# Two products and a convolution read from PSUM, and a softmax scaled on ScalarE instead of GpSimd, in a two-layer network

## The reference

```python
x = x + gla(xn) + local(xn)                  # xn = layernorm(x)
x = x + delta(xn) + moe(xn)                  # xn = layernorm(x)

# local attention, in windows of 64 queries, 8 heads, twice
attn = softmax(where(mask, -max, bq @ bk.T)); out = attn @ bv

# delta: short convolution, then per chunk of 32 tokens, for two gates w_l and w_g
q = silu(sum(xp[:, j:j + L, :] * w[:, j] for j in range(4)))      # k and v alike
u = T @ v_c;  wm = T @ kb_c
u_i = (u_i - wm_i @ S) * w_i[..., None]
o_i = q_i @ S + a @ u_i;  S = S + k_i.T @ u_i

# moe: 8 heads x 8 experts, gates from a top-2 routing
v = einsum('bshep,bshe->bhsp', x @ v_w, gate_v)
ctx = softmax(q @ k.T) @ v;  out = einsum over experts of (ctx * gate_o) @ o_w
```

## Time and profile before

| what | us |
|---|---|
| runs: median, lowest, highest | 1290.52, 1286.07, 1291.62 |
| the profiled execution | 1297.51 |
| its span | 1295.0 |
| PE, DVE busy | 1175.6, 971.2 |
| ACT, POOL busy | 721.9, 851.1 |

### The profile page before, as it was taken

The page is one execution under the profiler, slowest core; times in us unless marked ns, Lnnn a source line. Parts: engine busy times, 40 slices in busy tenths (PEclk is TensorE's granted clock), DMA queues, the critical chain, the costliest instruction groups (busy, mean ns, idle before and its releaser), DMA issues.

```text
span 1295.0 us, 31167 instructions
## 1 busy us (share of the span) xinstructions
PE 1175.6 (91%) x11890; PEld 930.8 (72%) x11890; DVE 971.2 (75%) x1950; ACT 721.9 (56%) x2060; POOL 851.1 (66%) x1157
## 2 busy tenths in 40 slices
PE   5778799899999798899999999989999898989898
PEld 3455477777678677777778777877688776878686
DVE  5858799876995969877687977968768956865354
ACT  5787876458655562567456665437666533332322
POOL 3746466686787727787568754887639876865841
PEclk9999989999999999999999999999999999999999
DMA  6111165555376438764566563775348565767673
GB/s 255 34 38 34 37 237 191 167 192 163 100 242 207 139 105 264 233 200 130 178 205 210 153 193 124 265 243 171 101 135 262 185 220 183 268 223 250 222 249 125
DMA packets 91186, 230.87 MB, mean 178 GB/s; under 512 B 9888, under 2 KB 16160, under 8 KB 90912
## 3 DMA queue, kind: packets, MB, share of 16 engines
q1 hardware_dynamic: 90896, 228.30, 54.3%
q10 hardware_dynamic: 144, 0.59, 0.1%
HBM read 225.71 MB, written 3.15 MB: 177 GB/s over the span
## 4 chain that ended last, share of the span: by engine, by line
PE 32%; DVE 24%; ACT 5%; DMA 4%; issue 3%; POOL 0%; DVEq 0%; ACTq 0%; POOLq 0%
PE bank L899 8%; PE bank L946 6%; DVE ogate L1352 5%; PE bank L827 3%; PE bank L936 2%; DVE dy L1210 2%; DVE kv L1123 2%; DMA kv<-values 2%; PE bank L612 2%; PE bank L917 1%; PE bank L927 1%; DVE mmin L1341 1%; PE bank L647 1%; DMA ogate<-gates 1%; PE bank L671 1%
## 5 line engine op out<-in xcount | busy, mean ns | idle before, releaser
L1748 POOL TENSOR_TENSOR vgate<-vgate,xT 128x512 f32<-128x512 f32 x256 | 330.3, 1313 | 102.4 <-DMA vgate<-gates 102.1
L899 PE MATMUL bank<-wv,vgate 128*128 128x128 f32 x2048 | 257.5, 280 | 6.4 <-DVE prob L1055 2.4
L899 PEld LDWEIGHTS bank<-wv,vgate 128*128 128x128 f32 x2048 | 245.3, 194 | 17.4 <-issue 5.2
L946 PE MATMUL bank<-ogate,wo 128*128 128x256 f32 x1024 | 244.4, 385 | 7.7 <-DVE ogate L1352 6.7
L946 PEld LDWEIGHTS bank<-ogate,wo 128*128 128x128 f32 x1024 | 189.8, 191 | 40.6 <-issue 14.3
L1352 DVE TENSOR_TENSOR ogate<-ogate,bank 128x1024 f32<-128x1024 f32 x128 | 152.9, 1212 | 33.3 <-PE bank L936 30.3
L1463 ACT ACTIVATE prob<-prob,mx 128x128 f32<-128x128 f32 (+1 forms) x256 | 96.0, 377 | 53.7 <-DVE mx L1059 53.4
L1681 POOL TENSOR_TENSOR rot<-rot 128x512 f32<-128x512 f32 x64 | 81.6, 1275 | 56.6 <-DVE rot L1035 56.2
L1630 ACT ACTIVATE mprob<-bank,mmin 128x256 f32<-128x256 f32 x128 | 59.2, 468 | 104.3 <-DVE mmin L1341 104.1
L1724 POOL TENSOR_TENSOR step<-dlt,uw 128x126 f32<-128x126 f32 (+22 forms) x248 | 92.5, 373 | 24.7 <-DVE dlt L1275 8.7
L1726 POOL TENSOR_TENSOR dlt<-dlt,step 128x126 f32<-128x126 f32 (+22 forms) x248 | 95.4, 385 | 19.4
(11 more groups left out here) (227 smaller groups left out, 2493.1 us busy)
## 6 DMA issues: line engine op xcount, KB each, us to landing
vgate<-gates SPq DMA_DIRECT2D x128, 512.0 KB, 4.5
ogate<-gates SPq DMA_DIRECT2D x128, 512.0 KB, 4.2
wv<-in_wv_moe SPq DMA_DIRECT2D x128, 256.0 KB, 4.8
wo<-in_wo_moe SPq DMA_DIRECT2D x128, 256.0 KB, 4.6
kv<-values SPq DMA_DIRECT2D x64, 256.0 KB, 4.5
local<-in_local SPq DMA_DIRECT2D x1, 1715.0 KB, 10.6
wqkv<-in_wqkv SPq DMA_DIRECT2D x2, 768.0 KB, 7.0
x<-in_x SPq DMA_DIRECT2D x8, 128.0 KB, 5.3
```

The lines of the kernel that those rows point to most:

```text
L899: i = nc.tensor.matmul(out[:, n * D:(n + 1) * D], xg[:, e, n * P:(n + 1) * P], m.wv[slot][:, e, :], start=(q, n, e) == (0, 0, 0), stop=(q, ...
L946: i = nc.tensor.matmul(out[:, 0:T], m.wo[slot][:, e, :], cg[:, e, :], start=(h, q, e) == (0, 0, 0), stop=(h, q, e) == (MH - 1, 1, EQ - 1))
L1748: i = tt(gate[:, e:e + half, :], gate[:, e:e + half, :], spread(m.xT[b % 2][:, :], 1, half), ALU.mult)
```

## The change

The convolution reads the products in their PSUM banks: DVE's first instruction multiplies the whole row by the last tap, and each later tap adds to the columns from 1, 2 or 3 on, so that neither `pad` nor its zeros are needed. ACT's three copies go; two products share a bank, so that `din` takes two banks instead of three. In the recurrence DVE multiplies `uw` by the gates' weights as it copies it from PSUM (w u - (w wm) S is w (u - wm S)), ACT's copy goes, and so does the second product of each chunk. The local softmax is scaled on ACT, by four instructions of one scale per row, where POOL had one multiplication. All turns and banks are written anew; the numbers of stages are the same, but for the pieces that come and go.

```diff
 TENSOR_TURNS = (
-    "GaaaaGGGaaaaabbXababbbbaGbababbabacaaacabGGbcacabGGcbbbaaabGbbaabbaaabbbGGaGcbGabcbbbcbcbGcbbGabaacaacGaaacbbc"
+    "GaaaaaGGGaaaaaGaaaaaXaabbababbbaabbbbaaababbabababbaacaGcbcabGbcbGababbbGbaaGbGaaaaabbGaabbaaabbabbcbbcbcbbbbc"
...
-         "fT": 1, "fsel": 1, "din": 3, "l2": 1, "dgate": 1, "kk": 1, "uw": 1, "du": 1, "ds": 1,
+         "fT": 1, "fsel": 1, "din": 2, "l2": 1, "dgate": 1, "kk": 1, "uw": 1, "du": 1, "ds": 1,
...
     def din(b):
-        for k in range(3):
-            bank = banks.of("din", b, i=k)
+        for i, kinds in enumerate(((0, 1), (2,))):
+            bank = banks.of("din", b, i=i)
             out = take(bank)
             x_ready(b)
-            nc.tensor.matmul(out[:, 0:T], m.w_delta[:, k, :], m.xT[b % 2][:, :], start=True, stop=True).then_inc(bank.filled, 1)
+            for at, k in enumerate(kinds):
+                last = nc.tensor.matmul(out[:, at * T:(at + 1) * T], m.w_delta[:, k, :], m.xT[b % 2][:, :], start=True, stop=True)
+            last.then_inc(bank.filled, 1)
...
     def conv(b, k):
-        raw = banks.of("din", b, i=k)
-        v.wait_ge(raw.emptied, raw.use)
-        v.wait_ge(s.zeroed1, 1)
+        bank = banks.of("din", b, i=k // 2)
+        raw, out = filled(bank)[:, k % 2 * T:(k % 2 + 1) * T], m.dy[b % 2][:, k, :]
...
-        v.chain(ts(m.dy[b % 2][:, k, :], m.pad[:, k, 0:T], m.conv[:, k, 0:1], None, ALU.mult))
-        for j in range(1, CONV):
+        v.chain(ts(out, raw, m.conv[:, k, CONV - 1:CONV], None, ALU.mult))
+        for late in range(1, CONV):
             v.settle()
-            i = stt(m.dy[b % 2][:, k, :], m.pad[:, k, j:j + T], m.conv[:, k, j:j + 1], m.dy[b % 2][:, k, :], ALU.mult, ALU.add)
-            if j < CONV - 1:
+            i = stt(out[:, late:], raw[:, 0:T - late], m.conv[:, k, CONV - 1 - late:CONV - late], out[:, late:], ALU.mult, ALU.add)
+            if late < CONV - 1 or k == 0:
                 v.chain(i)
-        i.then_inc(s.conv, 1)
+            else:
+                i.then_inc(bank.emptied, 1)
...
+    def uw(b, half):
+        bank = banks.of("uw", b, half)
+        v.wait_ge(s.dw, nth("dgates", b))
+        rows = m.uw[:, half * NC_:(half + 1) * NC_, :, :].rearrange("p c a t -> p c (a t)")
+        tt(rows, chunks(filled(bank)), spread(m.gates[b % 2][:, 2 + half, :], 2, 2 * CH), ALU.mult).then_inc(bank.emptied, 1)
...
         tt(m.dlt[:, c, :, :], u4[:, c, :, :], out, ALU.subtract).then_inc(bank.emptied, 1)
-        v.wait_ge(bank.emptied, bank.use)
-        tt(m.dlt[:, c, :, :], m.dlt[:, c, :, :], spread(m.gates[b % 2][:, 2:4, c], 2, CH), ALU.mult).then_inc(s.du, 1)
...
             e = act(p[:, c, :], p[:, c, :], ACT.Exp, scale=-1.0, bias=top[:, c:c + 1], accum_out=rsum[:, c:c + 1])
         e.then_inc(s.sexp, 1)
+        yield
+        a.wait_ge(s.ssum2, nth("score", b, l, w))
+        for c in range(LH // 2):
+            e = act(p[:, c, :], p[:, c, :], ACT.Copy, scale=rsum[:, c:c + 1])
+        e.then_inc(s.snorm, 1)
...
-    def din(b):
-        for k in range(3):
-            bank = banks.of("din", b, i=k)
-            act(m.pad[:, k, CONV - 1:], filled(bank)[:, 0:T], ACT.Copy).then_inc(bank.emptied, 1)
...
-    def uw(b, half):
-        bank = banks.of("uw", b, half)
-        act(m.uw[:, half * NC_:(half + 1) * NC_, :, :], filled(bank).rearrange("p (c a t) -> p c a t", c=NC_, a=2),
-            ACT.Copy).then_inc(bank.emptied, 1)
...
-    def score(b, l, w):
-        p, rsum = prob_of(m, b, l, w)[:, :, 0:keys_of(w)], sums_of(m, b, l, w)[1]
-        g.wait_ge(s.ssum2, nth("score", b, l, w))
-        tt(p, p, spread(rsum[:, :], 2, keys_of(w)), ALU.mult).then_inc(s.snorm, 1)
```

More of the change, by code:

```diff
@@ new lines @@
+    "VDDaVDDaDGAbbaDDVbbGaVbcbAaADGcVbbVbbDAcDPbbPbbAGGbEPcPcGAzAVaAVaaCaACPFPPAAVAVPPAcAAVAaVaaaaAFFCPPAAVaAaVGGDA"
+    "DGbDbDGcDPDDAAcbPcADDPFcbbbzPADVAAVCDDACbbDbPDDVDVDDAbbDAbAcCDDADVcDDGGVcDFcDADPPcEAAVAFFFPVAPaPaaaAAVAaPaVaAa"
+    "aAPAVAPaPaAbbAAaAPVPAbbAAVAaaDbbVDbaaAbaaabDGDVabbDVbaDDcGDDGbbPDcAADVADDVcbPAcDDGDcDDbDbbaDDbDPDDAAaVaADaVGbb"
+    "GAGGaDDPbbPbAcAVcAVcVPAPaPAcAVGAaPGcVAaAzAaEAVPPaVAGPAAabAaPGGbaAaGAAPAbVbPGCDVbbFAVAACDAbPbaDbFFFVaDPAabbAAGb"
+    "DDVcADPcDDGCDaADDcacDPbDDAbDaPcDbDDVDDaDVDDADzAPVbAbbDACVCPbbAEbAGDVVPAbbAbAVAcVcPAPFAAcVAVaPcaaaPPAcAAVCVGAaa"
@@ new lines @@
+    "aGcGcaaabcccaacbbzCCabbFFFCCCbCCFCCaAaCFFAaabGFFaabGGaaaFGGGGbabbcGGVVGGbaOOAacVAVGGacaVVDDcccOOAcbAzCDCbabaaC"
+    "CCbaVVOAOACCGGCbCcGbbVcVCbbcOObGVVbAFbAFFFOOcccVVcDAcAccOOaVaAVAaaGOOcccAcAaGaOOAFFbAaabbDDDGDFFbDGDbDFGGbaDaV"
+    "VGGDaDODaDODAGGAabDGaGbDVDVDaaDGGGGbVVbbGcGbGGDcDcbDVVbbADDbADOEGOcccacazOCOACAGVaVaCCCaaOCCOAFAVFVFCOOFACVAVC"
+    "aaFFcaaODOAAVGVDDDbDDbbcDGcDGGObGOGGGcAccDGFAFcFzbCDGbCOODVVACbDCbADCDCCCDVCVCDOcDODAcDAcVDVDFDcccFDFDDEcFOGOA"
+    "GFAFaFaFVVFaaOOaaAGGAGGVaaVGOaaOGAAbObbAOAabVVabODOAbAaDaVVDbDaabDaDaDVVDcDbGDbbcDObOAcDAVVccDcDGDcbDDbbDaDaOb"
@@ new lines @@
+GPSIMD_TURNS = (
+    "aaaaaaaaGGGaGaaGaGGaaGaaGaaaaaaGaaGGGGGGGaaaGaaaaaaaaaaaGaaGWWWGGWWWaaWaWaWGGDDaDaaWWaDGWDWDWWGDDDWWaWaWaaaGaa"
+    "aDDDDWaDaGDaDDWaDDGGaDGDDaWDaaWGDGWWGGWWDDDDDDWDWaWaWaaDWDaaaaGWWWDDDDGGGDDGDWWDDDDWWDDDDWWDDDDDaaWaaWDaaaaDWD"
+    "WDWGWaaaaGWaDaaDWaDGGDWDWDDDWWDDGDDDDaDaaWaWDaDDDGWGDGaGWaWaGWDGDGGDDaWaGaWaWWWDDaaDDDDDaaDWWDDWDDDDDWWWWDWWDD"
+    "WGDWDWaaGGGWaDaWaDaaWaGWDGDGaGWaWaWaDDDaDaDDaDaDDDWDDWDGDDaDaaaDDaDWDaaaDDWWDWDWWGGGWGWWWWDDWDDDWDWDGDGDDGWWDG"
+    "WDDDWDWWGWDWWDDDDDDDDWWWWDDDWDWDDWDDDWDWDDDWDDWDWDDDDDDDDWWWDDWWDDWDDWDWDDDDDDDD")
@@ L137 @@
+    "GGGoooovvovvvGGGGvoCoEvxovoovovovooovovvvvovvoovvGGGGGoovvvooovGGoGGvEvxoovooovovooGGGGGoCvvvoovvovvoExvvovvoo"
+    "vvooovCvGGGGoovvoovvooovvooGvGGGGvvoovEooovvoovvovvoovoCovvvGGoGGovvvovvovvvvvoooEoooovvoooovCvvvoovvvoovvoovo"
+    "EovvoooooovvvvvoooooE")
 BANK_TURNS = (
[L138 to L139 removed]
@@ new lines @@
+    "35043715471354715431413670364753104715437061430645305713045730415634054145310405314050154014531540317547313705"
+    "41327542730512735103721521720153172010052715321572731765217356721653267132673163571632313631215276521752617517"
+    "56217562167012515670321570627027310652713027153201731203415032431502450315423015203150423041240531240341043102"
+    "53042351014204124102410241064102641024130462104521074310742307162430742160372416307216340713647316374067340762"
+    "4367152340675320465732406573420735027605327056723065237")
@@ L493, in __init__ @@
         sb("fst", NT, 6), sb("fmv", NT, 2), sb("frstd", NT)
-        sb("pad", 3, CONV - 1 + T), pair("dy", 3, T)
+        pair("dy", 3, T)
         sb("dgT", 4, NC_, CH), sb("dg", 4, NC_), sb("dm", NC_)
@@ L870, in ds @@
     def ds(b, c):
-        bank = banks.of("ds", b, c)
+        bank, new = banks.of("ds", b, c), banks.of("du", b, c)
         out = take(bank)
-        pe.wait_ge(s.du, nth("du", b, c))
+        pe.wait_ge(new.emptied, new.use)
         per_head(out[:, 0:2 * CH], m.vkC[:, c, 1, :], flat(m.dlt[:, c, :, :]), start=True, stop=True).then_inc(bank.filled, 1)
@@ L1570, in fsel @@
         sigmoid(m.lp[:, :, :], m.lg[:, :, :], s.lp_raw)
-    def din(b):
-        for k in range(3):
-            bank = banks.of("din", b, i=k)
-            act(m.pad[:, k, CONV - 1:], filled(bank)[:, 0:T], ACT.Copy).then_inc(bank.emptied, 1)
     def silu(b):
-        a.wait_ge(s.conv, nth("conv", b, 2))
+        for i in range(2):
+            bank = banks.of("din", b, i=i)
+            a.wait_ge(bank.emptied, bank.use)
         sigmoid(m.de[:, :, :], m.dy[b % 2][:, :, :], s.silu)
@@ L1732, in du @@
     def du(b, c):
-        g.wait_ge(s.du, nth("du", b, c))
+        new = banks.of("du", b, c)
+        g.wait_ge(new.emptied, new.use)
         tt(m.dlt_sum[:, c, :], m.dlt[:, c, 0, :], m.dlt[:, c, 1, :], ALU.add).then_inc(s.dus, 1)
```

91 lines of the change are left out of this document (32 added, 59 removed).

## The result

The changed kernel takes 1256.05 us in the median of four runs (1253.31 to 1258.39), the kernel before 1291.07 beside it; the ratio is 0.9733, with 0.9698 to 0.9768 as its 95% interval. The forecast was 1281.2 with 1266 to 1300 for its range. The direction came out right; the size, -9 us for -35, was wrong, and the time lies outside the range. The profiled execution took 1255.72 us, of which 1254.4 are the span.

The account below looks back on a forecast made before the run. PE was taken to bound the kernel. DVE's relief -11.6, ACT's scaling +4.3 and +3.4, POOL -1.0 and the moved stages -4.4 sum to -9.3 us: from 1290.5 to 1281.2, range 1266 to 1300 (8 in 10).

Parts of the forecast that it names:

- What bounds: PE, busy for 91% of the span, bounds the kernel; no edit can gain more than its idle time, 119.4 us.
- The convolution and the recurrence: DVE's multiply-adds lose 20.0 us, first products 4.7, the chunks' second product 31.0; the gates' product from PSUM adds 10.9.
- DVE's relief: On the chain, convolution and recurrence sum to -15.5 us; three quarters kept, -11.6, with -7.8 and the whole as ends.
- DVE in sum: DVE's busy time over the whole kernel falls from 971.2 to 926.4 us.
- rival 3: ACT's work hidden, DVE's relief passes whole, POOL's relief holds DVE up less: 1269.6 us, PE idle below 100; chance 0.18.
- The softmax on ACT: Local softmax scaling moved from POOL to ACT: +4.3 us behind 405 us, +3.4 in the opening, -1.0 for POOL.
- The opening's part: In the first 141.6 us, ACT's 16.8 us of scalings for 13 windows count by a fifth, +3.4.
- The order: The new order of works, mostly left unpriced; only placing `l2`, `dgate` and `kk` early was counted, -4.4 us.
- one move: First batch's `l2`, two `dgate` and `kk` go before the first expert product, free in PE's idle time: -4.4 us.
- Rival 1: ACT becomes the bound and all its scalings in the opening delay PE: slower, 1299.0 us; chance 0.19.
- Rival 2: Convolution gains nothing: PSUM passes cost what they save, or the next held-up DVE instruction comes forward; 1289.0 us, chance 0.11.
- Rival 4: The new order is worse than the old one by more than the moved stages bring: 1286 us; chance 0.08.

Follow-up runs that it names:

- back_all: Changed kernel with all three edits (convolution, recurrence, softmax scaling) undone, its new order kept: 1317.6 us.
- copy_kept: Changed kernel with ACT's three copies of the convolution's inputs brought back and waited for by DVE, which still reads PSUM: 1274.3 us.

## Why the prediction was wrong, step by step

**What bounds.** Right that PE bounds. Wrong that no edit can gain more than PE's idle time: busy time gave 6 us too, by the clock.

**The convolution and the recurrence.** Their durations were nearly right: 20.0 us of multiply-adds forecast, 19.8 measured; 4.7 us of first products, 3.3 measured; 0.67 for 0.69. The term for DVE's relief, -11.6 (with ends at -7.8 and -15.5), is what the two edits bring in the old order: 1277.9 - 1290.7 = -12.8. The price by share of the chain held there. In the new order the same edits are worth 1317.6 - 1273.1 = 44.5. In the one place that was read, a held-up DVE instruction holds up ACT's queue, and with it a copy of another stage for which PE waits.

**DVE in sum.** 926.4 forecast, 900.9 measured. The further 25 us are in instructions that the change doesn't touch. The largest are two with two SBUF inputs, `dy<-dy,dgT` with 5.6 us less and `lc<-lc,layer` with 4.4, but some with one SBUF tensor and scalars per row are among them, `xn<-x,fmv,frstd` with 3.0. I supposed POOL's relief behind that in rival 3. The run with POOL's 62 us put back gives only 8.0 of DVE's busy time back (908.9); and back_all, with all the old instructions in the new order, has DVE at 935.0 for 971.2. So most of it is the order: which of POOL's pieces stand beside which of DVE's.

**The softmax on ACT.** +6.7 forecast, from +4.3 behind 405 us, +3.4 in the opening and -1.0 for POOL. In the old order it is +12.4 alone (1303.1) and +17.4 on top of the other two (1295.3 for 1277.9), so its sign was right for the order whose trace I read and its size about half of that. The opening's part, +3.4, is there about twice as large: the first expert product comes at 182.6 for 175.7 us. In the new order the edit is worth -17. Two prices failed by themselves, there at least: POOL's 62 us are worth 9.5, not 1.0, and ACT's, when doubled, 36 and not 8.

**The order.** This is the step that failed. "Most of it I can't price", and I set what I couldn't price at nothing and gave the order -4.4 for one move, as a term to be added to those of the edits. To the code with two edits the order brings 4.8 us, which looks like a hit but isn't clear of noise; to the code with all three it brings 39.2, and to the old code it costs 27. So there is no term for the order apart from the edits. That it pays only with the scaling on ACT in it suggests that it was drawn for that; no run shows it. The moved stages I had expected to be free; the opening became 13.6 us longer, 6.2 of them these stages, and the sum was won behind it.

**The direction.** It was luck in part. Without the order's term the forecast had -4.9 for the edits; in the order whose trace it was read from, they measure +4.6.

**The rivals.** Rival 3, the nearest, named 1269.6 and PE's idle time below 100 us as its mark; it is 84.8. It had the mark right and the mechanism in part: POOL's relief is 8.0 us of DVE's time. Rival 1 is what the old order would have done (1295.3, with 1299.0 named), and its mark, a first expert product at 185 or later with ACT busy over 85% ahead of it, half came true: 189 us and 81% (153.27 of 189), with the time on the other side. Rival 2 is refuted by the 482 ns. Rival 4, an order worse than the old one, is true of the old code (+27, if the placement is fair) and has the wrong sign for the changed one. The range was too narrow on the fast side because no case there was about the order.

**A rule weighed against the trace.** The Trainium skill, VectorE: DVE Perf Modes, section "Rules for kernel authors", offers the copy to SBUF first where many operations follow. Here four passes over PSUM cost 31 ns more than from SBUF in the first product and nothing in the multiply-adds (475 and 482 ns at the middle, against 444 and 486 before), and the copies, when VectorE waits for them, cost 18 us (copy_kept): the runs speak against the copy in this kernel.

## What to carry to other kernels

Where a change edits stages and redraws the order, read nothing from the old order's waits about the new one: build the old order with the edits, and the new order without them, as runs, and expect the corners of that table to differ by as much as the change itself or more. Look for what stands behind a waiting instruction in its queue, since that is who pays; here, at the place that was read, a slow convolution was paid by another stage's copy out of its bank. Don't take an engine with 0% of the chain for free (62 us of POOL cost 9.5), nor one with 5% for cheap twice (66 us of ACT cost 36).
